# Attention of eight heads in a twelve-layer kernel: one ring of three PSUM banks for every tile that ScalarE empties

## The chip, the cores and the metric

The kernel runs on one core of a Trainium2 chip. It is one program of twelve layers that follow one another on the core's engines: TensorE (PE in the profile, its weight loads PEld), VectorE (DVE), ScalarE (ACT), GpSimd (POOL) and SyncE (SP), which here only starts DMAs. The metric is the time of one execution on the device in microseconds, the median of several.

## The reference

Only the second layer, the cross-attention of the first block, matters here. `x1` is the layer-normalised state (32 sequences of 128 rows of 128 features), `x2` the context of the same shape; the result is added to the state.

```
def _L0_xattn_ref(x1, x2, Wq1, Wk1, Wv1, Wk2, Wv2, Wo, bo):
    h, d = (8, 64)
    scale = d ** (-0.5)
    q1 = split_heads(x1 @ Wq1, N1)
    k1 = split_heads(x1 @ Wk1, N1)
    v1 = split_heads(x1 @ Wv1, N1)
    k2 = split_heads(x2 @ Wk2, N2)
    v2 = split_heads(x2 @ Wv2, N2)
    k = jnp.concatenate([k1, k2], axis=1)
    v = jnp.concatenate([v1, v2], axis=1)
    sim = jnp.einsum('bihd,bjhd->bhij', q1, k) * scale
    attn = jax.nn.softmax(sim, axis=-1)
    out = jnp.einsum('bhij,bjhd->bihd', attn, v)
    out = out.reshape(B, N1, h * d)
    return out @ Wo + bo
```

## The kernel before

The layer is the function `attention8`. `NB` is 32 sequences, taken in `NG` = 8 groups of `GROUP` = 4. A step `s` handles one sequence, in two halves of four heads, numbered `g = 2 * s` and `g = 2 * s + 1`. Matrices are in fp32, and PE does each matrix product in two passes, so that the trace counts twice as many matmuls as the code.

What PE does, by the names in the code and the lines of the profile:

- `turn_h(j)` (L972): four transposes of the normalised state of group `j` into one bank.
- `project_qk(j, step)` (L979): one 128x512 fill; twelve of them make the queries and both sets of keys of group `j`. Step `s` of group `i` does three of the twelve fills of group `i + 1`, at `3 * u`, `3 * u + 1` and `3 * u + 2` (`u` is the step's place in its group). The first is of `wq`, the second of `wk1`, the third of `wk2`.
- `project_v(s, of_ctx)` (L984): one 128x512 fill, two for each sequence, made one step ahead.
- `scores(g)` (L996), `transposes(g)` of the probabilities (L1006, eight), `values(g)` (L1020) and `output(s)` (L1029, with `wo`).

DVE finds the maxima (`find_top`, L1190), divides the probabilities by their sums (`scale_probs`, L1194 and L1195) and copies the heads (`copy_heads`, L1203). ACT computes the exponents (`exponent`, L1119) and empties every other PSUM tile: the turned state (`copy_h`, L1101), queries (L1107) and keys (L1110), turned probabilities (`copy_turned`, L1128 and L1129), values (`copy_v`, L1133) and the output (`copy_output`, L1140). POOL adds the bias and the output to the state (L1230, L1232).

PSUM has eight banks. Before, the scores take four (`p_score0` and `p_score1`), the turned probabilities two (`p_trans`), the weighted values one (`p_pv`), and one bank, `p_misc`, takes turns for the turned state, all projections and the output. Each of these tiles has one or two semaphores of its own (`trans` and `h_t_ready`, `qk_done` and `qk_ready`, `v_done` and `v_ready`, `turned` and `turned_out`, `out_done` and `update_ready`).

The order on each engine is the order in which the code is written, and each engine takes its instructions in that order. In a step PE does: scores of the second half, output of sequence `s - 2`, the first fill of queries and keys, values of the last half before, the second fill, transposes of the first half, scores of the next step's first half, the first fill of `v`, values of the first half, transposes of the second half, the second fill of `v`, the third fill of queries and keys, and in each group's last step `turn_h` (for `i + 2 < NG`). ACT does, in this order: exponents of the first half, `copy_output(s - 2)`, the copy of the first fill, exponents of the second half, the copy of the second fill, the two copies of the turned probabilities, the copy of `v`, the two other copies of turned probabilities, the other copy of `v`, the copy of the third fill, and `copy_h`. Ahead of the steps stand `turn_h(0)`, the twelve fills of group 0, two fills of `v`, `turn_h(1)` and `scores(0)`. In the last group (`s` from 28) no queries and keys are projected any more.

What PE waits for ahead of a fill of `p_misc` is that ACT has copied what lay there, for example:

```
project_v(s + 1, 1)
if ahead:
    pe.wait_ge(v_ready, 2 * (s + 2))
    project_qk(i + 1, 3 * u + 2)
```

SP loads the context of a group (`c_t`, L961) when the group two before it is through, and right after the second group's load starts the loads of the next layer's weights.

## Time and profile before

| | us |
|---|---|
| median of three runs | 3437.21 |
| lowest and highest of the three | 3433.3 and 3439.65 |
| the profiled execution, whole | 3438.14 |
| its span in the trace | 3436.3 |
| PE busy in the span | 2560.0 |
| DVE busy | 2101.8 |
| ACT busy | 1392.5 |

The layer of the change lies between 449 and 933 us of the span: its context loads start at 449.38, and the loads that the next layer starts with are issued from 933.01 on. The profile's chain of work that ended last covers little of the span here, so the layer has to be read from its own stretch: from the busy times of the engines in it, from the list of waits, and from the timeline of one step. A matmul's busy time in the trace includes the time until its last column is out, which overlaps the next one; the distance between two starts says what a matmul costs in a row of them.

### The profile page before, as it was taken

The page shows a single profiled execution, that of the slowest core. Times are in us where ns is not written, and L with a number is a line of the kernel's source. Part 1 is how long each engine was busy: PE and PEld are TensorE (multiplying, and loading weights), DVE is VectorE, ACT ScalarE, POOL GpSimd, SP SyncE. Part 2 cuts the span into 40 slices and gives each one's busy share as a digit, 9 for nine tenths or more (in the row PEclk, how much of TensorE's full clock was granted, in tenths as well). Part 3 has the DMA queues.
Part 4 walks back from the last instruction along what each step waited for, and adds up shares of the span by engine and source line. Part 5 has one row for each costly group of instructions (what it writes and reads, how often), then busy time and mean ns, then how long its engine had stood idle before and what let it go on. Part 6 is the DMA issues. An engine that isn't in the chain of part 4 may idle for free. (4 is left out here: it accounts for less than half of the span.)

```text
span 3436.3 us, 53178 instructions
## 1 busy us (share of the span) xinstructions
PE 2560.0 (74%) x20516; PEld 1468.3 (43%) x20516; DVE 2101.8 (61%) x4141; ACT 1392.5 (41%) x2771; POOL 606.8 (18%) x581
## 2 busy tenths in 40 slices
PE   5777769888779889978887998688878953344361
PEld 3445435555534334434443444455553531222251
DVE  6888825444578554555654443677762227999757
ACT  4555526666523222212323443277832322444321
POOL 1342411111100033323430000111122021000003
PEclk8888869999989999988998998789979985777665
DMA  1000010000000000010000000200010110000010
GB/s 56 1 2 1 2 33 7 4 7 4 4 1 1 27 4 2 1 39 11 8 5 4 1 1 17 81 8 11 5 56 18 36 40 8 1 0 1 24 52 25
DMA packets 41988, 51.90 MB, mean 15 GB/s; under 512 B 9291, under 2 KB 30868, under 8 KB 40724
## 3 DMA queue, kind: packets, MB, share of 16 engines
q1 hardware_dynamic: 39700, 44.39, 4.1%
q0 software_dynamic: 2048, 4.20, 0.4%
q8 instruction: 164, 2.69, 0.3%
q14 instruction: 76, 0.62, 0.1%
HBM read 39.39 MB, written 9.18 MB: 14 GB/s over the span
## 5 line engine op out<-in xcount | busy, mean ns | idle before, releaser
L130 POOL TENSOR_TENSOR l_rstd<-l_moments,const_minus_half 128x4 f32<-128x4 f32 x104 | 118.3, 1138 | 1598.7 <-DVE l_moments L124 1572.2
L1407 PE MATMUL l_p_gate<-l_h_t,w_wg 128*128 128x512 f32 x400 | 208.4, 603 | 0.0
L1430 PE MATMUL l_p_out<-l_hidden,w_wd 128*128 128x512 f32 x400 | 204.4, 594 | 3.0 <-DVE l_hidden L1700 2.9
L2910 DVE SCALAR_TENSOR_TENSOR l_mix<-l_decay,l_cb 128x1024 f32<-128x1024 f32 x128 | 169.3, 1337 | 45.4 <-ACT l_decay L2793 42.9
L796 DVE TENSOR_REDUCE l_top<-l_ring 128x8 f32<-128x1024 f32 x128 | 150.7, 1220 | 69.4 <-PE l_ring L630 69.1
L2793 ACT ACTIVATE l_decay<-l_p_ring 128x1024 f32<-128x1024 f32 x128 | 130.2, 1031 | 148.2 <-PE l_p_ring L2683 146.7
L348 ACT ACTIVATE l_probs<-l_probs,l_minus_top 128x128 f32<-128x128 f32 x512 | 156.8, 392 | 55.8 <-DVE l_minus_top L407 55.7
L1190 DVE TENSOR_REDUCE l_minus_top<-l_p_score 128x4 f32<-128x1024 f32 x64 | 78.4, 1225 | 162.7 <-PE l_p_score L996 159.1
L1700 DVE TENSOR_TENSOR l_hidden<-l_act_out,l_p_spread 128x512 f32<-128x512 f32 x128 | 85.7, 685 | 128.9 <-ACT l_act_out L1528 128.7
L3170 PE MATMUL l_p_s<-const_ident,l_z 128*128 128x128 f32 x128 | 29.2, 423 | 179.4 <-ACT l_z L3209 179.4
L136 DVE TENSOR_SCALAR l_h<-x_res,l_moments,l_rstd 128x128 f32<-128x128 f32 (+1 forms) x384 | 112.4, 355 | 44.3 <-POOL l_rstd L130 44.0
L745 ACT ACTIVATE l_probs_t<-l_ring 128x1024 f32<-128x1024 f32 x64 | 62.0, 1021 | 165.0 <-PE l_ring L654 165.0
L745 ACT ACTIVATE l_probs_t<-l_ring,l_mask_col 128x1024 f32<-128x1024 f32 x64 | 67.8, 1110 | 146.2 <-PE l_ring L654 146.2
L1528 ACT ACTIVATE l_act_out<-l_p_gate,w_eb 128x512 f32<-128x512 f32 x128 | 85.5, 685 | 97.8 <-PE l_p_gate L1407 97.7
L881 POOL TENSOR_TENSOR l_spread_q<-l_q_t,const_slot_of 128x512 f32<-128x512 f32 x64 | 66.6, 1041 | 312.7 <-PE l_ring L654 312.7
L3329 DVE TENSOR_TENSOR l_srt<-l_srt 128x1024 f32<-128x1024 f32 (+3 forms) x112 | 115.9, 1035 | 9.7 <-ACT l_srt L3249 5.8
L1119 ACT ACTIVATE l_probs<-l_p_score,l_minus_top 128x256 f32<-128x256 f32 x256 | 118.1, 484 | 2.7 <-DVE l_minus_top L1190 2.7
L2698 PE MATMUL l_p_y<-l_mix,l_xdt_own 128*32 128x128 f32 x2048 | 92.1, 303 | 30.5 <-DVE l_mix L2910 26.9
L3330 DVE TENSOR_TENSOR l_srt<-l_srt 128x1024 f32<-128x1024 f32 (+3 forms) x112 | 114.8, 1025 | 0.0
L1430 PEld LDWEIGHTS l_p_out<-l_hidden,w_wd 128*128 128x128 f32 x400 | 75.3, 190 | 84.9 <-issue 52.3
L3170 PEld LDWEIGHTS l_p_s<-const_ident,l_z 128*128 128x128 f32 x128 | 26.2, 227 | 185.3 <-issue 155.9
L1407 PEld LDWEIGHTS l_p_gate<-l_h_t,w_wg 128*128 128x128 f32 x400 | 71.8, 192 | 77.6 <-issue 64.0
(473 smaller groups left out, 6315.3 us busy)
## 6 DMA issues: line engine op xcount, KB each, us to landing
l_c_t<-in_ctx_t SPq DMA_DIRECT2D x24, 256.0 KB, 2.7
l_rows_in<-l_zero SPq DMA_DIRECT2D x1, 2432.0 KB
l_tile_h<-l_rows_in SPq DMA_DIRECT2D x38, 64.0 KB, 1.9
l_rows_out<-l_tile_y SPq DMA_DIRECT2D x38, 64.0 KB, 1.5
w_mask<-in_mask SPq DMA_DIRECT2D x1, 2048.0 KB, 9.3
w_wg<-in_l2f_wg SPq DMA_DIRECT2D x1, 2048.0 KB
w_wu<-in_l2f_wu SPq DMA_DIRECT2D x1, 2048.0 KB
w_wd<-in_l2f_wd SPq DMA_DIRECT2D x1, 2048.0 KB
```

Of the source, the lines that this page charges most:

```text
L130: return nc.gpsimd.tensor_tensor(rstd[:, :], moments[:, :, 1], minus_half[:, 0:moments.shape[1]], ALU.pow)
L136: last = nc.vector.tensor_scalar(h[:, u, :], x[:, i * count + u, :], moments[:, u, 0:1], rstd[:, u:u + 1], ALU.subtract, ALU.mult)
L348: last = nc.scalar.activation(probs[:, g % 4, k, :], probs[:, g % 4, k, :], ACT.Exp, bias=minus_top[:, g % 4, k:k + 1])
L745: nc.scalar.activation(probs_t[:, b % 2, half * HALF:(half + 1) * HALF, :], turned_buffer(b, half)[:, :, :, :].rearrange("p a r q -> p (a ...
L796: nc.vector.tensor_reduce(top[:, b % 2, half * HALF:(half + 1) * HALF, 0], s, AX.X, ALU.max)\
L1119: last = nc.scalar.activation(probs[:, g % 2, k, :], p_score[g % 2][:, odd, b * KEYS:(b + 1) * KEYS], ACT.Exp, bias=minus_top[:, g % 2, k: ...
L1407: nc.tensor.matmul(p_gate[k % 2][:, :], w["wg"][:, s, :], h_t[:, g % 4, :], start=True, stop=True)\
L1430: nc.tensor.matmul(p_out[:, :], w["wd"][:, s, :], hidden[:, k % 4, :], start=(s == 0), stop=(gated and s == steps - 1)).then_inc(down, 1)
L2793: nc.scalar.activation(decay[:, g % RING, :, :], p_ring[slot % 2][:, :, :], ACT.Exp).then_inc(evicted, 1)
L2910: nc.vector.scalar_tensor_tensor(mix[:, g % RING, :, :], decay[:, g % RING, :, :], 1.0, bcast(cb[:, i % 2, n // 4, :], [T, QH, T], 1), ALU ...
L3329: nc.vector.tensor_tensor(da, a, b, ALU.max)
L3330: last = nc.vector.tensor_tensor(db, a, b, ALU.min)
```

## The change

`p_trans` and `p_misc` make way for `p_ring`, three banks of 128x512. Every tile that ACT empties is now a tile of this ring: the turned state, each fill of queries, keys or values, each output, and each half (a "pair" of heads, four transposes) of the turned probabilities. A table, `slot`, is filled ahead with the position of every such tile in the order in which PE fills them; tile `n` lies in bank `n % 3`. Two semaphores, `filled` and `evicted`, take the place of ten. PE waits ahead of tile `n` until tile `n - 3` is emptied, ACT waits ahead of its copy until tile `n` is full, and all who waited for one of the old semaphores wait for the position of the tile in question. The waits between the fills that stood for the single bank are gone. The order of the matmuls on PE and of the copies on ACT stays. `values` waits for `v` and for both pairs of its turned probabilities, the scores wait for the copy of the last fill of keys that they read, and the first fill of queries waits for the turned state.

The core of the diff:

```
-        p_trans = L.psum("p_trans", [T, 2, 4, T])
+        p_ring = [L.psum(f"p_ring{n}", [T, BANK]) for n in range(3)]
         p_pv = L.psum("p_pv", [T, 2, T])
-        p_misc = L.psum("p_misc", [T, BANK])
...
+        slot = {}
+
+        def takes(*tile):
+            slot[tile] = len(slot)
+
+        takes("h", 0)
+        for step in range(PER):
+            takes("qk", 0, step)
...
+            if s >= 2:
+                takes("out", s - 2)
+            if i + 1 < NG:
+                takes("qk", i + 1, 3 * u)
+                takes("qk", i + 1, 3 * u + 1)
+            takes("probs", 2 * s, 0)
+            takes("probs", 2 * s, 1)
+            if s + 1 < NB:
+                takes("v", s + 1, 0)
...
+                def ring(*tile):
+                    n = slot[tile]
+                    if n >= 3:
+                        pe.wait_ge(evicted, n - 2)
+                    return p_ring[n % 3]
...
                 def project_qk(j, step):
                     b, what = divmod(step, 3)
+                    if step == 0:
+                        pe.wait_ge(evicted, slot["h", j] + 1)
                     if what == 2:
                         pe.wait_ge(ctx_in[j % 2], 16 * (j // 2 + 1))
-                    nc.tensor.matmul(p_misc[:, :], (w["wq"], w["wk1"], w["wk2"])[what][:, b * T:(b + 1) * T],
-                                     (h_t, h_t, c_t)[what][:, j % 2, :], start=True, stop=True).then_inc(qk_done, 1)
+                    out = ring("qk", j, step)
+                    nc.tensor.matmul(out[:, :], (w["wq"], w["wk1"], w["wk2"])[what][:, b * T:(b + 1) * T],
+                                     (h_t, h_t, c_t)[what][:, j % 2, :], start=True, stop=True).then_inc(filled, 1)
...
                 def transposes(g):
                     pe.wait_ge(scaled, g + 1)
-                    if g >= 1:
-                        pe.wait_ge(turned_out, g)
-                    for k in range(8):
-                        last = nc.tensor.transpose(p_trans[:, k // 4, k % 4, :],
-                                                   probs[:, g % 2, k // 2, (k % 2) * T:(k % 2 + 1) * T],
-                                                   const["ident"][:, :])
-                    last.then_inc(turned, 1)
+                    for pair in range(2):
+                        out = ring("probs", g, pair)
+                        for k in range(4):
+                            last = nc.tensor.transpose(out[:, k * T:(k + 1) * T],
+                                                       probs[:, g % 2, 2 * pair + k // 2, (k % 2) * T:(k % 2 + 1) * T],
+                                                       const["ident"][:, :])
+                        last.then_inc(filled, 1)
...
                 turn_h(0)
-                pe.wait_ge(h_t_ready, 1)
                 for step in range(PER):
-                    if step:
-                        pe.wait_ge(qk_ready, step)
                     project_qk(0, step)
...
-                    if ahead and u == 0:
-                        pe.wait_ge(h_t_ready, i + 2)
-                    elif ahead:
-                        pe.wait_ge(qk_ready, PER * (i + 1) + 3 * u)
...
                     if ahead:
-                        if s >= 2:
-                            pe.wait_ge(update_ready, s - 1)
                         project_qk(i + 1, 3 * u)
...
                     if s + 1 < NB:
-                        pe.wait_ge(v_ready, 2 * (s + 1) + 1)
                         project_v(s + 1, 1)
                     if ahead:
-                        pe.wait_ge(v_ready, 2 * (s + 2))
                         project_qk(i + 1, 3 * u + 2)
...
                 def copy_turned(g):
-                    act.wait_ge(turned, g + 1)
                     if g >= 2:
                         act.wait_ge(weighed, g - 1)
-                    nc.scalar.copy(probs_t[:, g % 2, 0:4, :], p_trans[:, 0, :, :])
-                    nc.scalar.copy(probs_t[:, g % 2, 4:8, :], p_trans[:, 1, :, :]).then_inc(turned_out, 1)
+                    for pair in range(2):
+                        nc.scalar.copy(probs_t[:, g % 2, 4 * pair:4 * pair + 4, :], ring("probs", g, pair)[:, :])\
+                            .then_inc(evicted, 1)
```

How PE's row of instructions stands now. The words in brackets are semaphores by the name of the layer that had them first; a number is given back and used again by the next layer. Of the kernel before, `l0_dt_exp` is `v_ready`, `l0_own_ready` `update_ready`, `l0_dt_done` `qk_ready`, `l0_convolved` `h_t_ready`, `l0_cb_done` `turned_out`, `l0_x_turned` `scaled`, `l0_xs_half` `heads_ready`, `l0_high_ready` `expd` and `l0_stats_ready` a `ctx_in`. Of the changed kernel, `l0_filled` is `evicted`, `l0_da_ready` `scaled`, `l0_dt_in` `expd`, `l0_cum_done` `heads_ready` and `l0_stats_ready` a `ctx_in`.

PE of the kernel before, from the transposes of a step's second half to the next step's first fill of queries:

```order
L1006 MATMUL l1_p_trans<-const_ident,l1_probs 128x128 [waits l0_cb_done,l0_x_turned]
L1006 MATMUL l1_p_trans<-const_ident,l1_probs 128x128 x7
L984 MATMUL l1_p_misc<-w1_wv2,l1_c_t 128x512 [waits l0_dt_exp]
L979 MATMUL l1_p_misc<-l1_c_t,w1_wk2 128x512 [waits l0_stats_ready,l0_dt_exp]
L996 MATMUL l1_p_score1<-l1_keys,l1_q_t 128x256 [waits l0_high_ready,l0_dt_done]
L996 MATMUL l1_p_score1<-l1_keys,l1_q_t 128x256 x3
L1029 MATMUL l1_p_misc<-w1_wo,l1_heads_t 128x128 [waits l0_xs_half,l0_dt_done]
L1029 MATMUL l1_p_misc<-w1_wo,l1_heads_t 128x128 x3
L979 MATMUL l1_p_misc<-l1_h_t,w1_wq 128x512 [waits l0_own_ready]
```

PE of the changed kernel at the same place:

```order
L1040 MATMUL l1_p_ring0<-const_ident,l1_probs 128x128 [waits l0_filled,l0_da_ready]
L1040 MATMUL l1_p_ring0<-const_ident,l1_probs 128x128 x3
L1040 MATMUL l1_p_ring1<-const_ident,l1_probs 128x128 [waits l0_filled]
L1040 MATMUL l1_p_ring1<-const_ident,l1_probs 128x128 x3
L1018 MATMUL l1_p_ring2<-w1_wv2,l1_c_t 128x512 [waits l0_filled]
L1012 MATMUL l1_p_ring0<-l1_c_t,w1_wk2 128x512 [waits l0_filled,l0_stats_ready]
L1030 MATMUL l1_p_score1<-l1_keys,l1_q_t 128x256 [waits l0_dt_in,l0_filled]
L1030 MATMUL l1_p_score1<-l1_keys,l1_q_t 128x256 x3
L1064 MATMUL l1_p_ring1<-w1_wo,l1_heads_t 128x128 [waits l0_filled,l0_cum_done]
L1064 MATMUL l1_p_ring1<-w1_wo,l1_heads_t 128x128 x3
L1012 MATMUL l1_p_ring2<-l1_h_t,w1_wq 128x512 [waits l0_filled]
```

The order stays; consecutive tiles lie in different banks, each waits for the tile three before it, and the transposes have one more wait in their middle.

PE of the kernel before at the layer's start, the turned state and the first four fills:

```order
L972 MATMUL l1_p_misc<-const_ident,l1_h 128x128 x3
L979 MATMUL l1_p_misc<-l1_h_t,w1_wq 128x512 [waits l0_convolved]
L979 MATMUL l1_p_misc<-l1_h_t,w1_wk1 128x512 [waits l0_dt_done]
L979 MATMUL l1_p_misc<-l1_c_t,w1_wk2 128x512 [waits l0_stats_ready,l0_dt_done]
L979 MATMUL l1_p_misc<-l1_h_t,w1_wq 128x512 [waits l0_dt_done]
```

PE of the changed kernel there:

```order
L1002 MATMUL l1_p_ring0<-const_ident,l1_h 128x128 x3
L1012 MATMUL l1_p_ring1<-l1_h_t,w1_wq 128x512 [waits l0_filled]
L1012 MATMUL l1_p_ring2<-l1_h_t,w1_wk1 128x512
L1012 MATMUL l1_p_ring0<-l1_c_t,w1_wk2 128x512 [waits l0_filled,l0_stats_ready]
L1012 MATMUL l1_p_ring1<-l1_h_t,w1_wq 128x512 [waits l0_filled]
```

The second fill waits for nothing any more, and each later one for the copy three tiles back instead of the copy of the tile just before it.

## Rows read from the trace of the kernel before

**Rows 1.** The page: its first line, the span and the number of instructions.

```profile
span 3436.3 us, 53178 instructions
```

**Rows 2.** Busy time by stretch: stretch, length, five engines' busy us, granted clock, DMA.

```profile
500.00:880.00 380.00, 340.71 (x2249) 200.78 (x2250) 190.09 (x305) 241.53 (x720) 52.26 (x58) 1.00 0.02 5
```

**Rows 3.** Waits, 500 to 880 us: total us, times, longest us.

```profile
PE l_p_misc L979 <- ACT l_v L1133: 21.4, 27, 0.8
...
PE l_p_misc L979 <- ACT l_update L1140: 13.2, 26, 0.5
```

**Rows 4.** Timeline of one step: start us, us, engine, line, operation [idle before, releaser].

```profile
614.15 1.12 PE L984 MATMUL l_p_misc<-w_wv,l_h_t 128*128 128x512 f32 x2
...
616.23 1.09 PE L1006 MATMUL l_p_trans<-const_ident,l_probs 128*128 128x128 f32 x8
...
617.05 0.30 PEld L984 LDWEIGHTS l_p_misc<-w_wv,l_c_t 128*128 128x128 f32 x2
617.16 1.02 PE L984 MATMUL l_p_misc<-w_wv,l_c_t 128*128 128x512 f32 x2
...
618.32 0.60 ACT L1133 COPY l_v<-l_p_misc 128x512 f32<-128x512 f32 x1
...
618.98 1.12 PE L979 MATMUL l_p_misc<-l_c_t,w_wk 128*128 128x512 f32 x2 [0.79 <-ACT l_v L1133]
...
620.03 1.13 PE L996 MATMUL l_p_score<-l_keys,l_q_t 64*128 64x256 f32 x8
620.14 0.58 ACT L1110 COPY l_keys<-l_p_misc 128x512 f32<-128x512 f32 x1 [1.22 <-PE l_p_misc L979]
...
621.10 0.97 PEld L1029 LDWEIGHTS l_p_misc<-w_wo,l_heads_t 128*128 128x128 f32 x8 [0.33 <-ACT l_keys L1110]
621.10 1.16 PE L1029 MATMUL l_p_misc<-w_wo,l_heads_t 128*128 128x128 f32 x8
...
622.43 0.28 ACT L1140 COPY l_update<-l_p_misc 128x128 f32<-128x128 f32 x1
...
622.77 1.12 PE L979 MATMUL l_p_misc<-l_h_t,w_wq 128*128 128x512 f32 x2 [0.51 <-ACT l_update L1140]
...
622.80 1.52 DVE L1195 TENSOR_TENSOR l_probs<-l_probs,l_rec 128x1024 f32<-128x1024 f32 x1
...
623.82 1.09 PE L1020 MATMUL l_p_pv<-l_probs_t,l_v 128*64 128x128 f32 x16
...
625.81 1.04 PE L1006 MATMUL l_p_trans<-const_ident,l_probs 128*128 128x128 f32 x8
...
626.22 0.60 ACT L1110 COPY l_keys<-l_p_misc 128x512 f32<-128x512 f32 x1
...
627.84 1.12 PE L984 MATMUL l_p_misc<-w_wv,l_h_t 128*128 128x512 f32 x2
```

**Rows 5.** Timeline, 620 to 622.8 us: the second pass of the fill before the scores.

```profile
619.51 0.59 PE L979 MATMUL l_p_misc<-l_c_t,w_wk 128*128 128x512 f32 x1
```

**Rows 6.** Timeline of PE in a later layer, fills behind one another.

```profile
1975.08 1.02 PE L1430 MATMUL l_p_out<-l_hidden,w_wd 128*128 128x512 f32 x2
1975.93 1.02 PE L1407 MATMUL l_p_gate<-l_h_t,w_wg 128*128 128x512 f32 x2
```

**Rows 7.** Timeline of PE in a step that turns h.

```profile
605.76 0.66 PE L972 MATMUL l_p_misc<-const_ident,l_h 128*128 128x128 f32 x4 [0.68 <-ACT l_keys L1110]
606.35 1.13 PE L996 MATMUL l_p_score<-l_keys,l_q_t 64*128 64x256 f32 x8
```

**Rows 8.** Timeline, the layer's start: the first fill, the last, the first maximum.

```profile
455.13 2.07 PE L979 MATMUL l_p_misc<-l_h_t,w_wq 128*128 128x512 f32 x2 [0.73 <-ACT l_h_t L1101]
...
493.67 1.11 PE L972 MATMUL l_p_misc<-const_ident,l_h 128*128 128x128 f32 x4 [0.68 <-ACT l_v L1133]
...
496.84 1.23 DVE L1190 TENSOR_REDUCE l_minus_top<-l_p_score 128x4 f32<-128x1024 f32 x1 [38.68 <-PE l_p_score L996]
```

**Rows 9.** Busy time by half microsecond at the start: stretch, length, PE busy, granted clock.

```profile
498.00:498.50 0.50, 0.50 (x5) 0.97 0.00 0
```

More of the change, by code:

```diff
@@ L952, in attention8 @@
         UNITS8 = 2 * NB
-        head_at = lambda k: 2 * (k % 2) + k // 2
+        slot = {}
[4 more added lines that the diff above has]
+            takes("qk", 0, step)
+        takes("v", 0, 0)
+        takes("v", 0, 1)
+        takes("h", 1)
+        for s in range(NB):
+            i, u = divmod(s, GROUP)
+            if s >= 2:
[7 more added lines that the diff above has]
+                takes("v", s + 1, 0)
+            takes("probs", 2 * s + 1, 0)
+            takes("probs", 2 * s + 1, 1)
+            if s + 1 < NB:
+                takes("v", s + 1, 1)
+            if i + 1 < NG:
+                takes("qk", i + 1, 3 * u + 2)
+            if u == GROUP - 1 and i + 2 < NG:
+                takes("h", i + 2)
+        takes("out", NB - 2)
+        takes("out", NB - 1)
         with nc.Block() as block:
@@ L1027, in output @@
                     pe.wait_ge(heads_ready, 2 * (s + 1))
+                    out = ring("out", s)
                     for b in range(BLOCKS):
-                        last = nc.tensor.matmul(p_misc[:, 0:D], heads_t[:, s % 2, b, :], w["wo"][:, b, :],
+                        last = nc.tensor.matmul(out[:, 0:D], heads_t[:, s % 2, b, :], w["wo"][:, b, :],
                                                 start=(b == 0), stop=(b == BLOCKS - 1))
-                    last.then_inc(out_done, 1)
+                    last.then_inc(filled, 1)
                 turn_h(0)
-                pe.wait_ge(h_t_ready, 1)
                 for step in range(PER):
-                    if step:
-                        pe.wait_ge(qk_ready, step)
                     project_qk(0, step)
-                pe.wait_ge(qk_ready, PER)
                 project_v(0, 0)
-                pe.wait_ge(v_ready, 1)
                 project_v(0, 1)
-                pe.wait_ge(v_ready, 2)
                 turn_h(1)
@@ L1097, in _, with ring @@
                 act.wait_ge(at.loaded, at.count)
+                def ring(*tile):
+                    n = slot[tile]
+                    act.wait_ge(filled, n + 1)
+                    return p_ring[n % 3]
                 def copy_h(j):
-                    act.wait_ge(trans, j + 1)
-                    nc.scalar.copy(h_t[:, j % 2, :], p_misc[:, :]).then_inc(h_t_ready, 1)
+                    nc.scalar.copy(h_t[:, j % 2, :], ring("h", j)[:, :]).then_inc(evicted, 1)
                 def copy_qk(j, step):
                     b, what = divmod(step, 3)
-                    act.wait_ge(qk_done, PER * j + step + 1)
+                    out = ring("qk", j, step)
                     if what == 0:
-                        nc.scalar.activation(q_t[:, j % 2, b, :], p_misc[:, :], ACT.Copy, scale=float(HD8) ** -0.5)\
-                            .then_inc(qk_ready, 1)
+                        nc.scalar.activation(q_t[:, j % 2, b, :], out[:, :], ACT.Copy, scale=float(HD8) ** -0.5)\
+                            .then_inc(evicted, 1)
                     else:
                         nc.scalar.copy(keys[:, j % 2, b, :, (what - 1) * T:what * T],
-                                       p_misc[:, :].rearrange("p (u k) -> p u k", k=T)).then_inc(qk_ready, 1)
+                                       out[:, :].rearrange("p (u k) -> p u k", k=T)).then_inc(evicted, 1)
                 def exponent(g):
@@ L1115, in exponent @@
                     if g >= 2:
-                        act.wait_ge(turned, g - 1)
+                        act.wait_ge(filled, slot["probs", g - 2, 1] + 1)
                     for k in range(4):
```

56 lines of the change are left out of this document (19 added, 37 removed).

## Prediction

> **What bounds the kernel now.** The profiled execution took 3438.14 us, of which the trace spans 3436.3 [rows 1]; the 1.84 us around it stay. The change touches one layer, so the page's shares over the whole span say nothing, and I read the layer's own stretch. From 500 to 880 us PE is busy 340.71 of 380 us, ACT 241.53, DVE 190.09 and POOL 52.26, with a granted clock of 1.00 [rows 2]. PE is the one engine near its limit, and its missing 39 us are nearly all waits for ACT to empty `p_misc`: 21.4 us in 27 waits for the copy of `v`, 13.2 us in 26 waits for the copy of the output [rows 3]. The timeline of one step shows both: the third fill of queries and keys starts at 618.98 after 0.79 us of waiting, the first at 622.77 after 0.51 us [rows 4]. A step lasts 627.84 - 614.15 = 13.69 us. Ahead of the steps PE works by turns with ACT: from the first fill at 455.13 to `turn_h(1)` at 493.67 there are 14 fills, 38.54 us, 2.75 us each, of which 2.07 are PE's and 0.68 the wait for the copy [rows 8]. All of that passes at half clock: only at 498.0, 4.3 us into the first stretch without waits, does the granted clock reach 1.00 [rows 8, 9].
>
> **Third fill of each step.** The waits that the trace lists are not all that a stall costs. A fill that follows another without a stall has its weights loaded ahead: the loads for the second fill of `v` begin at 617.05 while the transposes still run, and its matmuls start at 617.16 [rows 4]. Such fills follow one another at 1975.93 - 1975.08 = 0.85 us although each is busy for 1.02 [rows 6], the passes at half of that, 0.43. After a stall the second pass comes 619.51 - 618.98 = 0.53 after the first [rows 4, 5]. So without the stall the third fill would start at 617.16 + 0.86 = 618.02, its second pass at 618.45, and the scores, which come 620.03 - 619.51 = 0.52 later, at 618.97: 1.06 us sooner than 620.03. That is 0.79 of idle time, 0.17 of a drain that is no longer waited out and 0.10 of a weight load. The step does it for `s` = 0 to 27: 28 x 1.06 = 29.7 us. (The step of `s` = 27 keeps a wait for its last keys, but gains the stall ahead of them.)
>
> **First fill of each step.** The output starts at 621.10 and its eight weight loads take 0.97. At the transposes the next matmul began 617.16 - 616.23 = 0.93 after the group's start, a little after its loads; by that the first fill would start 1.04 after the output, at 622.14, its second pass at 622.57, and the values 0.52 later at 623.09, 0.73 sooner than 623.82 [rows 4]. The wait exists from `s` = 2 on: 26 x 0.73 = 19.0 us.
>
> **Steps with `turn_h`.** Before, the third fill and the turned state are 1.80 apart (1.12 busy, 0.68 idle), and the scores follow 606.35 - 605.76 = 0.59 later, 2.39 in all [rows 7]. After, the turned state goes ahead in another bank, but the scores of the next group need the copy of the last keys. This wait is new there: the copy begins 1.06 after the fill's start (1.16 in the trace, less the weight load of 0.10), and PE starts 618.98 - 618.32 = 0.66 after a copy's start [rows 4], 1.72 in all. That saves 0.67, of which 0.10 is counted above: 6 x 0.57 = 3.4 us.
>
> **The start.** With a ring of three the fills no longer wait for ACT: a copy takes 0.60, less than any spacing of fills. At full clock a fill costs 0.86, at half clock twice that, 1.72. The work from the first fill on is then one unbroken stretch, and the clock rose 4.3 us into such a stretch [rows 8, 9]. I take three fills at half clock and eleven at full: 5.2 + 9.4 = 14.6 instead of 38.5, which saves 23.9 us. If the clock never rose it would be 24.1, and save 14.4. The first maximum follows `turn_h(1)` by 496.84 - 493.67 = 3.17 us at half clock [rows 8]; at full clock the turn costs 0.59 [rows 7] and the scores 1.13 to their end, some 1.8 together, 1.4 us less.
>
> **The end.** The last `values` wait for both copies of the turned probabilities. The first of these can now start when four of eight transposes are done, half of 0.93 earlier; two such places save 0.9 us, with zero as the other bound. In the steps from 28 on, PE waits for DVE's division and nothing of that moves.
>
> **What the change adds.** A second wait and a second increment in each of 64 groups of transposes. I take them at zero, as the second fill of `v`, which also carries a wait that was met long before, had its weights loaded without a gap [rows 4]. The other bound is the load that is not pulled ahead, 0.10 each, 6 us in all. The Trainium skill (TensorE: Matmul & The Clock Gate, "The cost: per-tile semaphore tail") states 26.3 ns for every increment more; by that figure the sum would be 1.7 us smaller, and no row here has the price. No instruction changes engine or place, no DMA is issued later or behind anything new.
>
> **What is late next.** I laid the shortened step out from the scores' start as 0: output 1.07, first fill 2.11, values 3.07, second fill 4.10, transposes 5.06, scores 6.02, fill of `v` 7.09, values 8.14, transposes 9.17, fill of `v` 10.10, third fill 10.96, end 11.90. DVE's division ended at 622.80 + 1.52, that is 4.29 after the scores' start [rows 4]; the transposes want it at 5.06, 0.77 later. The first fill of `v` needs the bank of the second fill, whose copy stands on ACT behind the second half's exponents: it started 6.19 after the scores [rows 4], some 0.7 sooner in the new step as the first fill's copy comes sooner, and is done at 6.2, with 0.9 to spare. The third fill needs the first pair of transposes emptied: full at 9.9, emptied at 10.5, with 0.4 to spare. That is the tightest place. No wait for the ring should last, and PE bounds the step at 11.90 us, with ACT's work of 241.53 / 380 x 13.69 = 8.7 beside it [rows 2].
>
> **Sum.** 29.7 + 19.0 + 3.4 + 23.9 + 1.4 + 0.9 = 78.3 us. The profiled execution would be 3438.1 - 78.3 = 3359.8 us. The median of the runs shown, 3437.21, is 0.9 below that execution, which I neglect.
>
> **Rivals.** First, **loads wait with their fill**: a wait on the ring might keep weight loads from being pulled ahead. Then only listed idle time goes: 28 x 0.79 + 26 x 0.51 + 6 x 0.33 (0.68 less the new wait) = 37.4 us, a fill at the start costs its busy time (3 x 2.07 + 11 x 1.12 = 18.5, saving 20.0), and with 1.4 and 0.9 the gain is 59.7: 3378.4 us. Against it speaks the load at 617.05. Second, **the clock stays at half through the start**: 52.1 + 14.4 + 0.9 = 67.4, 3370.7 us. For it speaks that the 14 fills, at 2.07 of 2.75 us, never raised it in 38 us; against it, that a gap of 0.68 us stood behind each of those and stands behind none now.
>
> Third, and slower: **the clock falls in the steps**. PE would run through banks in turn, stop shortly at the ring and drop to half clock again and again. At half clock a fill takes 2.07 instead of 1.12, and a step of 11.9 us that PE fills costs up to 11.9 more; so from 78.3 / 11.9 = 6.6 such steps on, the change is a loss, and with ten of the 28 the time would be 3359.8 + 119 = 3479 us. Against it: the clock was 1.00 for 380 us with more and longer gaps [rows 2]. The Trainium skill names the mechanism (TensorE: Matmul & The Clock Gate, "A second HAM failure mode: psum-queue depth-cycling"): a kernel that cycled through PSUM banks each iteration idled shortly between groups of matmuls, and its clock went up and down between the two levels. By that rule the time would be the 3479 just worked out; the trace disagrees so far. Fourth, **the ring doesn't free PE**: another in-order wait on ACT eats what the fills gain in the steps, and only start and end gain: 26.2 us, 3411.9 us. It takes the place of a wait only if ACT is more than 1 us late at three places in each step, against the slacks above.
>
> **How the numbers follow.** The forecast has a chance of 0.74, loads with their fill 0.12, the slow start 0.07, the ring that doesn't free PE 0.03, the falling clock 0.03, a change without effect 0.01. Around the forecast I allow 8 us each way for the load in the transposes, the size of the first fill's gain and the runs' own spread of 6. With the first two rivals that gives 3349 to 3381 us. A measurement of this kernel can tell about 0.2%, 7 us. Faster by more than that has 0.96, within it 0.01, slower 0.03.
>
> **What the profile after would show.** A step of 11.9 us between 500 and 850 us, PE busy above 97% there, no wait of PE for the copy of `v` or the output, only one of about 0.3 for the last keys in each fourth step. Fills at the start spaced 1.72 and then 0.86 us, the clock at 1.00 before 463. The layer ends at about 855 us instead of 933. Wrong would be: a step above 12.3 us with waits for ACT at the third fill or the fill of `v`, a row of transposes with a gap in its middle, or fills spaced at 1.12.

## The result and the profile of the changed kernel

| | before | changed |
|---|---|---|
| median of the runs on one chip, us | 3438.43 | 3353.74 |
| lowest and highest | 3433.3 and 3440.0 | 3351.46 and 3359.67 |
| the profiled execution, whole | 3438.14 | 3355.69 |
| its span | 3436.3 [rows 1] | 3353.8 |

The ratio is 0.9759 (95% interval 0.9741 to 0.9776), 82.4 us less in the profiled executions. The forecast was 3359.8 us for the profiled execution; the median lies 6.1 below it.

The changed kernel's busy times, in the columns of [rows 2], for the stretch in which its steps run:

```profile
500.00:850.00 350.00, 342.59 (x2414) 215.42 (x2412) 194.01 (x305) 253.39 (x758) 57.14 (x63) 1.00 0.02 6
```

PE is busy 98% of it, where it was 90% before. Its waits in the same stretch, as in [rows 3]:

```profile
PE l_p_ring L1040 <- DVE l_probs L1207: 3.9, 4, 1.1
...
PE l_p_score L1030 <- ACT l_keys L1124: 2.1, 7, 0.7
```

The 27 waits for the copy of `v` and the 26 for the output's copy are gone. PE waits for the last keys in seven places, 2.1 us together, and for DVE's division in the steps of the last group. These last steps, and what follows them up to the last output, are called the drain. One step in the timeline, PE alone (start, busy, operation, idle before), to be held against [rows 4]:

```profile
579.80 1.13 PE L1030 MATMUL l_p_score<-l_keys,l_q_t 64*128 64x256 f32 x8
580.87 1.16 PE L1064 MATMUL l_p_ring<-w_wo,l_heads_t 128*128 128x128 f32 x8
581.86 1.02 PE L1012 MATMUL l_p_ring<-l_h_t,w_wq 128*128 128x512 f32 x2
582.82 1.09 PE L1054 MATMUL l_p_pv<-l_probs_t,l_v 128*64 128x128 f32 x16
...
588.91 1.09 PE L1040 MATMUL l_p_ring<-const_ident,l_probs 128*128 128x128 f32 x8
589.85 1.02 PE L1018 MATMUL l_p_ring<-w_wv,l_c_t 128*128 128x512 f32 x2
590.71 1.02 PE L1012 MATMUL l_p_ring<-l_c_t,w_wk 128*128 128x512 f32 x2
591.66 0.70 PE L1030 MATMUL l_p_score<-l_keys,l_q_t 64*128 64x256 f32 x4
```

There is no idle time in it, and the step is 591.66 - 579.80 = 11.86 us, against 13.69. From the output to the values it is 582.82 - 580.87 = 1.95, against 2.72 in [rows 4]; from the transposes to the scores 591.66 - 588.91 = 2.75, against 3.80. The layer's start answers to [rows 8], and under it DVE's first maximum:

```profile
454.64 2.07 PE L1012 MATMUL l_p_ring<-l_h_t,w_wq 128*128 128x512 f32 x2 [0.73 <-ACT l_h_t L1115]
456.50 1.91 PE L1012 MATMUL l_p_ring<-l_h_t,w_wk 128*128 128x512 f32 x2
458.21 1.91 PE L1012 MATMUL l_p_ring<-l_c_t,w_wk 128*128 128x512 f32 x2
459.92 1.06 PE L1012 MATMUL l_p_ring<-l_h_t,w_wq 128*128 128x512 f32 x2
460.81 1.02 PE L1012 MATMUL l_p_ring<-l_h_t,w_wk 128*128 128x512 f32 x2
...
469.40 0.60 PE L1002 MATMUL l_p_ring<-const_ident,l_h 128*128 128x128 f32 x4
```

```profile
471.11 2.35 DVE L1202 TENSOR_REDUCE l_minus_top<-l_p_score 128x4 f32<-128x1024 f32 x2 [13.44 <-PE l_p_score L1030]
```

Three fills are 1.71 to 1.86 apart, the next 0.86 to 0.89, and the clock has risen by the fourth, at 459.92.

Two places went another way than forecast. In the first step, and at the end of the drain, some of the matmuls take nearly twice their time. Both pieces are PE alone:

```profile
475.82 1.09 PE L1040 MATMUL l_p_ring<-const_ident,l_probs 128*128 128x128 f32 x8 [1.99 <-DVE l_probs L1207]
476.85 1.92 PE L1030 MATMUL l_p_score<-l_keys,l_q_t 64*128 64x256 f32 x8
478.70 1.98 PE L1018 MATMUL l_p_ring<-w_wv,l_h_t 128*128 128x512 f32 x2
480.61 1.09 PE L1054 MATMUL l_p_pv<-l_probs_t,l_v 128*64 128x128 f32 x16
```

```profile
843.76 1.09 PE L1040 MATMUL l_p_ring<-const_ident,l_probs 128*128 128x128 f32 x8 [1.10 <-DVE l_probs L1207]
845.68 1.97 PE L1054 MATMUL l_p_pv<-l_probs_t,l_v 128*64 128x128 f32 x16 [0.83 <-ACT l_probs_t L1142]
847.58 1.81 PE L1040 MATMUL l_p_ring<-const_ident,l_probs 128*128 128x128 f32 x8
850.12 1.09 PE L1054 MATMUL l_p_pv<-l_probs_t,l_v 128*64 128x128 f32 x16 [0.72 <-ACT l_probs_t L1142]
```

The granted clock of the first of them (last but two of the columns):

```profile
477.00:477.50 0.50, 0.50 (x4) 0.42 (x6) 0.50 (x1) 0.50 (x3) 0.00 (x0) 0.55 0.00 0
477.50:480.00 2.50, 2.50 (x8) 0.96 (x6) 1.77 (x2) 0.55 (x2) 0.00 (x0) 0.50 0.00 0
```

PE idles 1.99 us for DVE's division, works some 1.2 us at full clock, and then has half clock, from inside the stretch of 0.55 until past 480.00, while it is busy without a pause. A second profile of the changed kernel has both places again (scores of 1.93 us, values of 1.98), and so has the kernel with more waits below.

Where the 82.4 us lie, from the starts of the same instruction in both traces:

| stretch | before | changed | less | forecast |
|---|---|---|---|---|
| up to the layer's first transposes | 453.31 | 452.82 | 0.5 | 0 |
| first fill to `turn_h(1)` | 38.54 | 14.76 | 23.8 | 23.9 |
| `turn_h(1)` to the scores behind the first transposes | 8.91 | 7.45 | 1.5 | 1.4 |
| step 0 | 6.95 | 7.53 | -0.6 | 1.1 |
| step 1 | 12.02 | 10.96 | 1.1 | 1.1 |
| steps 2 to 27 | 364.64 | 313.41 | 51.2 | 49.9 |
| from step 28 to the next layer's first transposes | 52.65 | 52.98 | -0.3 | 0.9 |
| all behind it, to the end of the span | | | 5.3 | 0 |

The layer as a whole, from its first transposes to those of the next, went from 485.53 to 408.91 us. The experiments are read by this length, since it is free of what other layers do: it repeats to 0.04 us in a second profile of either kernel, while the untouched part behind it took anything from 2472 to 2509 us in the twelve profiles. Its first part, up to `turn_h(1)`, is called the start (40.36 and 16.58 us).

### The profile page after: what moved, and what is told of

The parts are those of the page before. It is cut to its first block and busy times, and to the rows that moved or that the text cites. A ratio compares the mean times of both kernels' runs of the same rounds, so it can differ in the third digit from the quotient of the medians.

```text
span 3353.8 us, 53186 instructions
## 1 busy us (share of the span) xinstructions
PE 2526.7 (75%) x20516; PEld 1467.6 (44%) x20516; DVE 2096.9 (63%) x4141; ACT 1392.8 (42%) x2771; POOL 607.7 (18%) x581
```

## The experiments

The first four ran on one chip, where the kernel before took 3421.26 us. The next three, and the kernel before once more, ran on another (3435.02), all three edits in one kernel and the changed kernel once more on a third (3447.4). Each is an edit of the changed kernel, unless it says otherwise. With each, the ratio to the kernel before on its chip is given.

**The third fill waits again, and nothing else.** It waits for the tile just ahead of it.

```
                     n = slot[tile]
-                    if n >= 3:
+                    if tile[0] == "qk" and tile[1] >= 1 and tile[2] % 3 == 2:
+                        pe.wait_ge(evicted, n)
+                    elif n >= 3:
                         pe.wait_ge(evicted, n - 2)
```

> The changed kernel with one wait put back: the third fill of queries and keys in each step waits until the tile just before it (the second fill of v) is emptied, as in the kernel before. Theory: the stall costs 1.06 us per step, namely 0.79 of idle time, 0.17 of a drain waited out and 0.10 of a weight load that is not pulled ahead; the step goes from 11.85 to 12.91 us, the layer is 28 x 1.06 = 29.7 us longer than in the changed kernel. Rival (only the idle time that the waits list counts): 12.64 us per step, 22 us in all.

The layer took 435.59 us, 26.7 more; ratio 0.9826 (0.9809 to 0.9842). PE in one of its steps:

```profile
596.36 1.09 PE L1042 MATMUL l_p_ring<-const_ident,l_probs 128*128 128x128 f32 x8
...
599.08 1.10 PE L1014 MATMUL l_p_ring<-l_c_t,w_wk 128*128 128x512 f32 x2 [0.77 <-ACT l_v L1148]
600.11 1.13 PE L1032 MATMUL l_p_score<-l_keys,l_q_t 64*128 64x256 f32 x8
```

The listed idle time is 0.77, yet the transposes and the scores are 600.11 - 596.36 = 3.75 apart instead of 2.75: the stall costs 1.00, not 0.77. In a step with `turn_h` it is 1.01 too (4.50 from the transposes to the scores, against 3.49). Over 28 fills this would be 28.1. The layer grew by 1.4 less, and that lies in its drain, where this kernel has no half clock behind the same waits:

```profile
870.33 1.09 PE L1042 MATMUL l_p_ring<-const_ident,l_probs 128*128 128x128 f32 x8 [1.10 <-DVE l_probs L1209]
...
875.19 1.09 PE L1056 MATMUL l_p_pv<-l_probs_t,l_v 128*64 128x128 f32 x16 [0.83 <-ACT l_probs_t L1144]
```

From one row to the other it is 4.86 us, in the changed kernel 850.12 - 843.76 = 6.36. So a stall in front of a fill costs more than its idle time, by about what the forecast put down to the last matmul's own drain and to a weight load, and the reading by listed idle time (0.77 x 28 = 21.6) falls. The whole program got less slower than the layer: 17 us in the medians against the kernel with six more waits on this chip, whose layer is that of the changed kernel. The part behind the layer, the same code in both, was 9.5 us shorter in this kernel's profile.

**The start waits again, and nothing else.** Each tile up to `turn_h(1)` waits for the one just ahead.

```
-                    if n >= 3:
+                    if 1 <= n <= slot["h", 1]:
+                        pe.wait_ge(evicted, n)
+                    elif n >= 3:
                         pe.wait_ge(evicted, n - 2)
```

> The changed kernel with the waits of the layer's start put back: each tile up to the second turned state waits until the tile just before it is emptied. Theory: the 14 fills from the first to the second turned state take 38.5 us again instead of 14.8, at a granted clock of 0.50, and the scores behind them run at half clock, 25.3 us more; the steps stay at 11.85 us. The dip of the clock in the first step (half clock from 477.2 to 480.2 in the changed kernel), which costs 1.64 us, may or may not come. Rival (the clock rises by itself after some time whatever PE does): fills at 1.05 + 0.68 = 1.8 us from about the fifth on, some 15 us more.

The layer took 432.86 us, 23.95 more; its start took 24.2 more (40.78, against 16.58) and the rest 0.25 less; ratio 0.9836 (0.9820 to 0.9853). Its last fill, PE alone:

```profile
491.96 2.08 PE L1020 MATMUL l_p_ring<-w_wv,l_c_t 128*128 128x512 f32 x2 [0.68 <-ACT l_v L1148]
```

Up to the last of the 14 fills each has its wait and half the clock. The clock rises where the waits are gone, not with time: the rival that it would rise by itself falls. In this kernel the first step has no half clock. PE idles 1.52 us there, up to the first transposes, and what follows runs at full. That saves 1.6 us, and the scores of the start, still at half clock, cost 1.4 more, so the two cancel nearly. The drain has its half clock as in the changed kernel. The first step:

```profile
502.66 1.10 PE L1042 MATMUL l_p_ring<-const_ident,l_probs 128*128 128x128 f32 x8 [1.52 <-DVE l_probs L1209]
503.69 1.14 PE L1032 MATMUL l_p_score<-l_keys,l_q_t 64*128 64x256 f32 x8
```

**Two banks instead of three.**

```
-        p_ring = [L.psum(f"p_ring{n}", [T, BANK]) for n in range(3)]
+        p_ring = [L.psum(f"p_ring{n}", [T, BANK]) for n in range(2)]
...
-                    if n >= 3:
-                        pe.wait_ge(evicted, n - 2)
-                    return p_ring[n % 3]
+                    if n >= 2:
+                        pe.wait_ge(evicted, n - 1)
+                    return p_ring[n % 2]
```

> The changed kernel with a ring of two banks instead of three, otherwise the same order and table. Theory: by the laid-out step the second pair of transposes of the first half now waits for the copy of the second fill (0.65 us late, and a weight load), the second fill of v for the copy of the first pair (0.4 us late), and the third fill starts with its weights not loaded ahead: a step of 13.1 to 13.4 us instead of 11.85, about 28 x 1.4 = 39 us more, and 1 to 3 us more at the start, where a copy is done just as the second next fill could begin. Rival (a second bank is all that matters, the third is spare): 11.85 to 12.0 us per step.

The layer took 446.09 us, 37.2 more, of which 0.6 in the start; ratio 0.9863 (0.9846 to 0.9879). The places at which PE waits in a step of 606.45 - 593.35 = 13.10 us:

```profile
593.35 1.13 PE L1030 MATMUL l_p_score<-l_keys,l_q_t 64*128 64x256 f32 x8
...
598.35 0.60 PE L1040 MATMUL l_p_ring<-const_ident,l_probs 128*128 128x128 f32 x4
599.42 0.66 PE L1040 MATMUL l_p_ring<-const_ident,l_probs 128*128 128x128 f32 x4 [0.47 <-ACT l_keys L1124]
...
604.54 1.13 PE L1018 MATMUL l_p_ring<-w_wv,l_c_t 128*128 128x512 f32 x2 [0.29 <-ACT l_probs_t L1142]
...
606.45 0.49 PE L1030 MATMUL l_p_score<-l_keys,l_q_t 64*128 64x256 f32 x2
```

Two banks already bring nearly all of the start: 0.6 us are missing there, where 1 to 3 were expected. In the steps the group of transposes needs both, and its second half waits for the copy of the fill ahead of it. The third bank is worth 13.10 - 11.86 = 1.24 us a step, more than half of what the ring as a whole gives there (1.83).

**Six satisfied waits more in each group of transposes.** The forecast took the added waits at nothing and named 0.10 each as the other bound. The edit puts a wait ahead of each of the eight; ahead of two of them the ring's own wait stands already.

```
                         for k in range(4):
+                            pe.wait_ge(evicted, slot["probs", g, pair] - 2)
                             last = nc.tensor.transpose(
```

> The changed kernel with six more waits in each group of eight transposes, one ahead of each transpose, on a count that is always reached long before. Theory: a wait that is met costs PE nothing, the weights are loaded ahead all the same: step 11.85 us, no difference. Rival (a wait keeps the load from being pulled ahead, 0.10 us each): up to 2 x 6 x 0.10 = 1.2 us per step, 38 us in all.

The layer took 408.91 us, the same to the hundredth; ratio 0.9772 (0.9756 to 0.9789). In this kernel 384 waits more, met long before, cost nothing. The added increment can be read in the changed kernel itself: the transposes with two increments and the fill behind them are 589.85 - 588.91 = 0.94 apart in the rows above, with one increment they were 0.93 [rows 4], and the difference is rounding. Over all such groups between 500 and 800 us the distance is 0.930 on average in both kernels (22 groups before, 25 after). The 26.3 ns for each increment that the Trainium skill gives (TensorE: Matmul & The Clock Gate, "The cost: per-tile semaphore tail") would be 1.7 us for the layer. They don't show here. The Trainium skill gives the figure there for matmuls that run side by side in the array and whose increments queue up, while here the two increments are half a group apart.

**Work for PE where it idled.** Matmuls whose result nobody reads, at the idle place of the first step and in the drain. They add work to the kernel, and its output doesn't use them.

```
+                    if s == 0:
+                        for _ in range(4):
+                            nc.tensor.matmul(p_pv[:, :, :], const["ident"][:, :], h_t[:, 0, 0:2 * T], start=True, stop=True)
                     transposes(2 * s)
+                    if s == NB - 1:
+                        for _ in range(2):
+                            nc.tensor.matmul(p_score[0][:, 0, 0:2 * T], const["ident"][:, :], h_t[:, 0, 0:2 * T], start=True, stop=True)
```

> The changed kernel with matmuls whose result nobody reads, in two places where PE idles and the clock then falls: four of 256 columns ahead of the first step's first transposes (an idle time of 1.99 us), two ahead of the last sequence's first values (0.83 us). Theory: the two stretches at half clock (477.2 to 480.2 and 845.7 to 849.1 in the changed kernel) follow from these idle times; filled, the clock stays at 1.00, the first step is 1.6 us shorter, the end about 1 us, the layer 406.3 instead of 408.9 us from its first PE work to the next layer's. Rival (the fall has nothing to do with the gap): both dips stay and the layer keeps 408.9 us or grows by up to 0.6 us.

The layer took 405.77 us, 3.1 less; ratio 0.9776 (0.9758 to 0.9794). PE in the first step:

```profile
475.26 1.89 PE L1090 MATMUL l_p_pv<-l_h_t,const_ident 128*128 128x256 f32 x8
477.41 1.09 PE L1040 MATMUL l_p_ring<-const_ident,l_probs 128*128 128x128 f32 x8 [0.26 <-DVE l_probs L1213]
478.43 1.13 PE L1030 MATMUL l_p_score<-l_keys,l_q_t 64*128 64x256 f32 x8
```

The added matmuls fill the gap from 475.26 on, the idle time in front of the transposes falls from 1.99 to 0.26, and the scores take 1.13 instead of 1.92. The transposes themselves come no sooner, since DVE sets them. What was lost in the first step was the half clock that came behind the gap, not the gap. The step is 5.89 us now, 1.06 less than before the change. The drain is 1.49 us shorter too, but it is so as well in three kernels without added matmuls there (third fill waiting, matmuls in front of the layer, two fills exchanged), so this run doesn't show that they were the cure in the drain.

**Work for PE in front of the layer.** The same kind of unread matmuls ahead of the first transposes, and one behind them, so that the clock stands at full before the first fill. Nothing reads them either.

```
+                for _ in range(4):
+                    nc.tensor.matmul(p_pv[:, :, :], const["ident"][:, :], w["wq"][:, 0:2 * T], start=True, stop=True)
                 turn_h(0)
+                nc.tensor.matmul(p_pv[:, 0, :], const["ident"][:, :], w["wq"][:, 0:T], start=True, stop=True)
```

> The changed kernel with matmuls whose result nobody reads while PE waits for the layer's first normalised state: four of 256 columns ahead of the first turned state and one of 128 columns behind it, where PE waits for its copy. Theory: the clock rises some 4 us after the first of them, ahead of the first fill or with it, instead of in the fourth fill; the 14 fills take 12.0 to 13.5 us instead of 14.8, and the layer is 1.5 to 3 us shorter. Rival (the clock rises at its old moment): nothing is gained, and the matmul of 128 columns costs up to 0.1 us.

The layer took 404.50 us, 4.4 less, with a start of 13.69; ratio 0.9752 (0.9735 to 0.9770). PE at the start:

```profile
444.81 3.75 PE L1069 MATMUL l_p_pv<-w_wq,const_ident 128*128 128x256 f32 x8 [9.52 <-PEq L41]
...
449.28 0.39 PE L1071 MATMUL l_p_pv<-w_wq,const_ident 128*128 128x128 f32 x2
450.18 1.12 PE L1012 MATMUL l_p_ring<-l_h_t,w_wq 128*128 128x512 f32 x2 [0.51 <-ACT l_h_t L1118]
```

All 14 fills run at full clock, 12.12 us from the first to `turn_h(1)` against 14.76. It brought more than expected: 2.9 in the start, and 1.5 in the drain, where nothing was changed (see the sum below). The first step keeps its 1.99 us of idle time and its half clock (scores of 2.08 us).

**The third fill of keys ahead of the second fill of `v`,** in the table, on PE and on ACT, so that the last keys are copied sooner.

```
+                    if ahead:
+                        project_qk(i + 1, 3 * u + 2)
                     if s + 1 < NB:
                         project_v(s + 1, 1)
-                    if ahead:
-                        project_qk(i + 1, 3 * u + 2)
```

> The changed kernel with the third fill of queries and keys ahead of the second fill of v, on PE, on ACT and in the table. Theory: the last keys of a group are then emptied while PE fills v, so that the waits ahead of the next group's first scores go, 0.24 us in six steps and 0.68 in one; the steps stay at 11.85 us, the layer is 2.1 us shorter. Rival (the keys' fill now comes too soon behind the transposes, whose first pair has to be emptied for it): the fill waits 0.4 us in each of 28 steps and the layer is some 9 us longer.

The layer took 405.42 us, 3.5 less; ratio 0.9778 (0.9762 to 0.9794). A step with `turn_h`, first of the changed kernel, then of this one, PE alone:

```profile
615.27 0.60 PE L1002 MATMUL l_p_ring<-const_ident,l_h 128*128 128x128 f32 x4
616.11 1.13 PE L1030 MATMUL l_p_score<-l_keys,l_q_t 64*128 64x256 f32 x8 [0.24 <-ACT l_keys L1124]
```

```profile
615.37 0.60 PE L1002 MATMUL l_p_ring<-const_ident,l_h 128*128 128x128 f32 x4
615.90 1.13 PE L1030 MATMUL l_p_score<-l_keys,l_q_t 64*128 64x256 f32 x8
```

The 2.1 us of waits for the last keys are gone, which gives 2.0 of the 3.5, and the other steps stay at 11.85. The other 1.5 are the half clock in the drain, which is gone too although nothing was changed there, and the waits of about the same lengths still stand:

```profile
842.46 1.09 PE L1040 MATMUL l_p_ring<-const_ident,l_probs 128*128 128x128 f32 x8 [1.11 <-DVE l_probs L1207]
...
847.33 1.09 PE L1054 MATMUL l_p_pv<-l_probs_t,l_v 128*64 128x128 f32 x16 [0.83 <-ACT l_probs_t L1142]
```

From the first of these rows to the last it is 4.87 us, against the 6.36 of the changed kernel: the half clock costs 1.49 there.

**All three in one kernel.**

> The three edits of the last group in one kernel: unread matmuls in front of the layer's first transposes and one behind them, unread matmuls in the idle stretch of the first step and in the drain, and the third fill for queries and keys in front of the second fill for values. Alone they took 4.4, 3.1 and 3.5 us from the layer. Theory (each cures its own place: the start 2.9, the dip of the clock in the first step 1.6 or more, the drain 1.4, the fourth steps 2.0): the layer is 408.9 - 8 = about 401 us, start 13.7, rest 387 to 387.5, and the ratio to the kernel before is about 0.2% lower than that of the changed kernel on the same chip. Rival (the three share the same stretches of half clock, and one of them pays for all): the layer is 404 to 405 us, the same as with one alone.

The layer took 400.85 us, 8.1 less, with a start of 13.69: the theory's number. Alone the three give 3.14 + 4.41 + 3.49 = 11.04; each of them had also moved the drain's 1.49, which is to be had once, and 11.04 - 2 x 1.49 = 8.06. Against the kernel before it is 0.9749 (0.9725 to 0.9773), five executions from 3353.8 to 3365.6 us. The changed kernel beside it is at 0.9772, so the median gained only 0.2%, and the two intervals overlap: that the whole program is faster by these 8 us is not shown.

**The kernel before, and the changed kernel, once more.** They ask where the 5.3 us behind the layer come from. The trace has 4.6 of them in the fifth layer, which no edit touches: 286.7 us before, 282.2 after.

> The kernel before once more, for the lengths of the untouched layers. Between the first pair of profiles the fifth layer (from its first mask matmul to the sixth layer's first router matmul) was 286.7 us before and 282.1 us after, though its code is the same. Theory: it varies from run to run with the moment at which the clock rises and falls, and now falls anywhere between 282 and 287. Rival (the changed layer ahead of it makes it shorter, by the moment at which it starts): 286.7 again. The changed layer itself takes 485.5 us from its first PE work to the next layer's, both times.

> The changed kernel once more, on the chip of the run beside it. Theory (the layer's time doesn't depend on the chip): layer 408.9 us, start 16.6, rest 392.3; the fifth layer 282.1 to 282.7 us, against 286.7 and 286.8 in the two profiles of the kernel before. Rival (the fifth layer varies from execution to execution, and the 4.6 us there were chance): it comes out nearer to 287.

The kernel before took 286.7 us in that layer again, with 485.49 us for the layer of the change, and the changed kernel 282.2, with 408.93. So this difference isn't chance from one execution to the next. The 5.3 us as a whole are another matter: from the next layer's first transposes to the end of the span it was 2497.5 and 2492.1 us in the first pair of profiles, 2506.0 and 2504.1 in the second, only 1.9 apart, because other untouched layers differ the other way.

And the fifth layer doesn't go with the change alone. The seven experiments before the last one took 282.2 to 282.7 us in it, but the kernel with all three edits, which has the change in it, took 286.2. One group of matmuls of that layer, with the same idle time ahead of it in all three kernels (before, changed, all three edits):

```profile
1560.43 2.09 PE L651 MATMUL l_ring<-l_spread_q,l_k_t 32*128 32x512 f32 x8 [2.82 <-DVE l_top L796]
```

```profile
1482.02 1.14 PE L651 MATMUL l_ring<-l_spread_q,l_k_t 32*128 32x512 f32 x8 [2.82 <-DVE l_top L796]
```

```profile
1475.64 2.09 PE L651 MATMUL l_ring<-l_spread_q,l_k_t 32*128 32x512 f32 x8 [2.82 <-DVE l_top L796]
```

After the same 2.82 us of idle time the granted clock is at half in the first and the third, and at full in the second. The 5 us around it show it too, in the same order (columns as in [rows 2]):

```profile
1559.00:1564.00 5.00, 3.57 (x16) 1.30 (x16) 2.41 (x3) 0.00 (x0) 0.00 (x0) 0.56 0.01 3
```

```profile
1481.10:1486.10 5.00, 3.99 (x61) 2.22 (x61) 2.94 (x4) 1.98 (x2) 1.85 (x2) 1.00 0.01 3
```

```profile
1474.50:1479.50 5.00, 3.86 (x17) 1.45 (x17) 2.12 (x2) 0.00 (x0) 0.00 (x0) 0.50 0.02 3
```

From the layer's mask matmuls ahead of this group to the next ones it is 11.35, 8.71 and 11.23 us, so over half of the 4.6 us lie here. The change needn't make that layer faster, then; what differs is whether the clock falls at such a place. What decides that is not settled, and that the moved start decides it is not shown: the layer starts at 1534.0, 1456.2 and 1449.5 us in the three, but the kernels that start it at 1448.1 (matmuls in front of the layer) and 1453.5 (two fills exchanged), on either side of the third, took 282.7 and 282.2. No run here varies that moment alone.

## Why the prediction was right

The mechanism was the forecast one: PE bound the layer, its waits for one shared bank were what it lost, and with three banks ACT's copies lie behind other work of PE. 76.6 us of the forecast 78.3 came out of the layer. Point by point:

- **Third fill of each step**, forecast 1.06 x 28. The timeline has 1.05, from 3.80 to 2.75, and undoing this part alone cost 1.00 to 1.01 in each step. That a stall costs more than its listed idle time was the step on which 7.6 us of the sum hung, and it holds.
- **First fill of each step**, forecast 0.73 x 26. It was 0.77: the fill follows the output after 0.99 us, not after the 1.04 that I had taken from the transposes. This term was sized 1.0 us too small. No run puts this wait back alone; the 0.77 rests on the two timelines.
- **Steps with `turn_h`**, forecast 3.4 in all. Steps 2 to 27 gained 51.2 us; 26 x 1.84 (13.69 less 11.85) is 47.8 of it, and 3.4 are left. This too is read from the traces. The new wait for the last keys is there, 0.24 instead of 0.35.
- **The start**, forecast 23.9, measured 23.8, with three fills at half clock and eleven at full, as laid out; the clock was at full from 460 on, and the forecast had said before 463. The rival of a clock that stays at half falls, and the run with the old waits at the start shows that it is the waits that hold it there.
- **First maximum**, 1.4 forecast; `turn_h(1)` to the maximum is now 1.71 instead of 3.17, so 1.46.
- **Step 0** was sized wrongly, and its mechanism was not in the forecast. It was to give 1.1 and cost 0.6, 1.6 us off in all. From the first maximum to the first transposes it is 4.7 us in both kernels (501.56 - 496.84 and 475.82 - 471.11), so DVE and ACT set them in both. PE is ready for them 2 us sooner after the maximum than it was, as its second fill no longer waits for ACT (1.19 us in the trace of before) and its scores run at full clock; so it idles for 1.99 us, and half clock followed. With that gap filled the step gave the 1.06 of the forecast. I had laid out the step of the middle, where DVE's division is 0.77 early, and not the first one, where it is late.
- **The end**, forecast 0.9 with zero as the other bound, came out at -0.3, outside both. The two places at which `values` wait for the first copy did gain: 1.92 from the transposes to the values instead of 2.25 (923.79 - 921.54 in the trace of before), 0.33 each, where 0.45 was forecast. Some 0.5 more came from shorter waits for DVE (1.10 instead of 1.22 a step, where the forecast let nothing move) and for the last output's copy. In the kernels without half clock there this stretch is 51.49 us, 1.16 less than before. The half clock in the drain took 1.49 back. The bound of zero was no bound, for I had taken the clock as settled once it was at full.
- **What the change adds**: nothing, by the run with 384 more waits. The bound of 0.10 each can be dropped.
- **The rivals.** Loads that wait with their fill: falls by the spacing of 0.86 and by the first experiment. The ring that doesn't free PE: falls by the 98%. The falling clock: between 500 and 850 us it is 1.00, with ten tiles a step that go through all three banks in turn. The Trainium skill (TensorE: Matmul & The Clock Gate, "A second HAM failure mode: psum-queue depth-cycling") ties a clock that goes up and down to such cycling with short pauses of PE between the groups of matmuls. In the steps the traces don't show it: there is no pause with three banks, and with two banks, where PE waits 0.47 and 0.29 us in a step, the clock is 1.00 as well. Half clock came at two other places, each once in an execution, behind idle times of 0.8 to 2 us, and cost 3.1 us together.

Against the profiled execution the forecast was 4.1 us too long. 1.7 us less than forecast came from the layer: the half clock took 3.1, and terms sized too small (the first fill, the end) gave about half of it back, which is luck. 5.8 us came from outside the layer, which the forecast had at nothing. 4.6 of them are in the fifth layer and repeat, the sum doesn't: in the second pair of profiles the part behind the layer differs by 1.9. So the sum was nearer than the time, and part of the 8 us that I allowed was needed for something I hadn't named: the layers behind it don't keep their length.

## What to carry to other kernels

Where an in-order engine fills tiles that another one empties, count how many tiles lie between a fill and its copy, over all kinds of tiles together; one ring with a table of positions gives each the same distance, and two banks gave nearly all of the start, three were needed in the steps. Price a stall by the distance between two starts with and without it, not by the idle time that the trace lists: here it was 1.05 for 0.79. And when a stretch gets shorter, look again at its edges, where an engine that was just in time is now waited for, and where half clock may follow that wait.

## What the runs showed of the hardware

- Half clock can come behind an idle time, when PE has been back at work for some 1.2 us: idle until 475.82, the transposes then at full (1.09 us), at half from 477.50 to 480.00 while PE was busy without a pause. The idle time alone doesn't decide it. Behind 1.98 to 1.99 us in the first step it came in each of the six kernels with that idle time, and behind 1.52 us in one kernel nothing fell; behind the same 2.82 us the clock was 1.00 in one and half in two; and the drain's pauses of 1.1 and 0.83 us were followed by half clock in the changed kernel (both profiles), in the one with more waits and in the one with the old start, but not in the one with two fills exchanged, in the one with matmuls in front or in the one whose third fill waits.
- Matmuls that nobody reads kept the clock up over the gap of the first step, and raised it ahead of the layer. In front of the layer they were worth 2.6 us for its 14 fills, though PE did 4.1 us more work, in time in which it had been idle (3.75 and 0.39).
- An untouched layer took 286.7 us in both profiles of the kernel before, 282.2 to 282.7 in nine profiles of kernels with the change, and 286.2 in a tenth. A difference of 0.1% between two versions of this kernel can be that alone.
